# First attention of a four-layer chain: two heads share 128 rows, batches see only their own keys, query norms turned one tile later

## What is computed

```python
q = (hidden @ q_proj_w.T)   # 32 heads of 128
k = (ctx @ k_proj_w.T)      # 8 key/value heads of 128
v = (ctx @ v_proj_w.T)
q = rmsnorm(q, q_norm_w); k = rmsnorm(k, k_norm_w)       # per head
scores = einsum('bhqd,bhkd->bhqk', q, repeat(k, 4)) * scale + attention_mask
attn = softmax(scores)
out = einsum('bhqk,bhkd->bhqd', attn, repeat(v, 4))
return out @ o_proj_w.T
```

## Time and profile before

| | us |
|---|---|
| median of 3 runs | 2617.65 (2617.49 to 2620.02) |
| span of the profiled execution | 2617.0 |
| first attention in it, first projection matmul to last x update | 79.6 to 737.8 |
| TensorE busy, share of the span | 88% |
| VectorE, ScalarE, GpSimd busy | 52%, 45%, 20% |
| granted TensorE clock, mean of the span | 0.954 |

### The profile page before, as it was taken

One profiled execution on the slowest core, in us unless ns is written; L12 is line 12 of the kernel. 1 busy time (PEld: TensorE's weight loads), 2 busy tenths in 40 slices (PEclk: granted clock), 3 DMA queues, 4 the chain that ended last, 5 costly groups with the idle time before them and its releaser, 6 DMA issues.

```text
span 2617.0 us, 40130 instructions
## 1 busy us (share of the span) xinstructions
PE 2310.4 (88%) x14092; PEld 1295.4 (49%) x14108; DVE 1352.7 (52%) x2614; ACT 1167.1 (45%) x2986; POOL 530.5 (20%) x875
## 2 busy tenths in 40 slices
PE   0789989899977777999999999999769899999979
PEld 0455555555543333455555555555534455555545
DVE  2466666666652024465555565555342455555551
ACT  2455556565511112554554554543122555555530
POOL 1233332332220001122222222211200111221120
PEclk9999999999978888999999999999879999999988
DMA  3111011010000111111111111100210010000000
GB/s 126 35 41 42 22 42 37 26 41 17 1 21 14 83 71 50 59 59 43 61 60 43 61 60 43 61 11 11 77 64 1 33 49 33 32 32 32 1 29 33
DMA packets 27172, 108.74 MB, mean 42 GB/s; under 512 B 4305, under 2 KB 12881, under 8 KB 16866
## 3 DMA queue, kind: packets, MB, share of 16 engines
q1 hardware_dynamic: 26978, 106.24, 11.5%
HBM read 104.13 MB, written 2.10 MB: 41 GB/s over the span
## 4 chain that ended last, share of the span: by engine, by line
PE 58%; ACT 15%; DVE 14%; issue 10%; POOL 1%; DMA 1%; ACTq 0%; DVEq 0%; POOLq 0%; SPq 0%
PE bank L84 14%; PE bank L85 14%; PE bank L86 14%; DVE m_Sm L785 2%; ACT m_E L409 2%; PE bank L1222 2%; DVE m_x L831 2%; PE bank L1551 2%; ACT m_E L405 2%; PE bank L579 2%; ACT m_arena L387 2%; DVE m_nmax L801 1%; ACT m_arena L297 1%; PE bank L1131 1%; PE bank L1336 1%
## 5 line engine op out<-in xcount | busy, mean ns | idle before, releaser
L725 DVE TENSOR_TENSOR m_arena<-bank,m_arena 128x512 f16<-128x512 f32 x336 | 232.1, 691 | 541.6 <-ACT m_arena L387 541.2
L84 PE MATMUL bank<-m_input_parts,m_arena 128*128 128x512 f16 x1088 | 416.8, 383 | 9.5 <-DVE m_input_parts L694 2.8
L85 PE MATMUL bank<-m_input_parts,m_arena 128*128 128x512 f16 x1088 | 416.4, 383 | 0.4 <-issue 0.4
L86 PE MATMUL bank<-m_input_parts,m_arena 128*128 128x512 f16 x1088 | 416.4, 383 | 0.0
L409 ACT ACTIVATE m_E<-m_Sm,m_nmax 128x128 f32<-128x128 f32 x512 | 199.1, 390 | 427.4 <-DVE m_nmax L801 251.6
L843 POOL TENSOR_TENSOR m_E<-m_E,m_rinv 128x512 f32<-128x512 f32 x192 | 199.9, 1041 | 917.6 <-DVE m_rinv L816 917.6
L84 PE MATMUL bank<-m_wo_t,m_A 128*128 128x512 f16 x768 | 295.0, 384 | 34.5 <-DVE m_x L831 34.5
L387 ACT ACTIVATE m_arena<-bank 128x512 f16<-128x512 f32 x336 | 198.9, 592 | 243.7 <-PE bank L86 243.3
L85 PE MATMUL bank<-m_wo_t,m_A 128*128 128x512 f16 x768 | 294.3, 383 | 0.0
L86 PE MATMUL bank<-m_wo_t,m_A 128*128 128x512 f16 x768 | 293.6, 382 | 0.0
L405 ACT ACTIVATE m_E<-bank,m_nmax,m_qk 128x128 f32<-128x128 f32 x256 | 113.8, 454 | 195.1 <-DVE m_nmax L774 195.1
(11 more groups left out here) (258 smaller groups left out, 4454.5 us busy)
## 6 DMA issues: line engine op xcount, KB each, us to landing
m_raw<-a_q SPq DMA_DIRECT2D x24, 1024.0 KB, 4.8
m_raw<-a_o SPq DMA_DIRECT2D x24, 1024.0 KB, 4.9
m_raw<-a_k SPq DMA_DIRECT2D x9, 1024.0 KB, 4.9
m_raw<-a_v SPq DMA_DIRECT2D x9, 1024.0 KB, 5.4
m_bias_in<-bias SPq DMA_DIRECT2D x64, 128.0 KB, 2.0
m_arena<-ctx_t SPq DMA_DIRECT2D x3, 2048.0 KB, 7.8
m_arena<-f_w SPq DMA_DIRECT2D x4, 1024.0 KB, 5.1
m_arena<-ctx SPq DMA_DIRECT2D x1, 2048.0 KB, 8.1
```

The lines of the kernel that those rows point to most:

```text
L84: pe.matmul(out, lhs[0], rhs[0], start=first, stop=False)
L85: pe.matmul(out, lhs[0], rhs[1], start=False, stop=False)
L86: return pe.matmul(out, lhs[1], rhs[0], start=False, stop=last)
L725: ins = dve.tensor_tensor(self.dest(name, part, 1), self.shaped(bank[m % 2][:, :]), self.dest(name, part, 0), ALU.subtract)
```

## The change

In the first attention two heads of one batch share the 128 rows of a score block, and each block has only the 64 keys of its own batch. A unit then has four blocks of 128 by 64 (two batches by two pairs of heads) in place of four of 128 by 128. Queries, their squares and the mixed output are laid out by batch and pair of heads, as the last attention already does it (`self.packed`). The mask is 128 by 64. Two transposes are made in place of four. The values lie in two copies, each with zeros in the rows of the other batch, and the mix is two products of 256 columns. The value tile is split by two operations of 64 rows on ScalarE and on VectorE. GpSimd clears the values once in the setup; the mask's two loads no longer wait. And in the list of events `q_turn` moves behind the slot's `tile`.

```diff
@@ events
             if normed == 3:
-                out.append(("q_turn", misc, slot // 4))
-                misc += 1
                 out.append(("k_scale", slot // 4))
             if todo:
                 out.append(("tile", todo.pop(0), slot // 4))
+            if normed == 3:
+                out.append(("q_turn", misc, slot // 4))
+                misc += 1
@@ ScalarE, tile
+                    if self.layer == 0 and name[0] == "V":
+                        for q in range(2):
+                            own = slice(q * S, (q + 1) * S)
+                            ins = act.activation(k.V[own, 0, part, q, :], src[own, :], ACT.Copy)
+                        ins.then_inc(s["proj_hi"].sem, 1)
+                        continue
@@ ScalarE, scores and turn
-                        cols = slice(h * P, (h + 1) * P)
+                        cols = slice(h * self.keys, (h + 1) * self.keys)
-                    act.activation(k.PT[:, b % 2, 0, :], bank[4][:, :], ACT.Copy).then_inc(s["turned_hi"].sem, 1)
+                    act.activation(self.pt_dst(b, 0), bank[4][:, 0:self.keys * HG], ACT.Copy).then_inc(s["turned_hi"].sem, 1)
@@ TensorE, scores
+                        if self.packed:
+                            b2, hp = (j // 2, j % 2) if self.layer == 3 else (j % 2, j // 2)
                             lhs = [k.q3[:, i, hf, hp, pt * 2 + b2].rearrange("p h n -> p (h n)") for i in range(2)]
+                                rhs = [k.K[:, i, hf, 0, (pt * 2 + b2) * S:(pt * 2 + b2 + 1) * S] for i in range(2)]
-                        ins = mm3(pe, out[:, j * P:(j + 1) * P], lhs, rhs)
+                        ins = mm3(pe, out[:, j * self.keys:(j + 1) * self.keys], lhs, rhs)
@@ TensorE, turn and mix
-                    for j in range(4):
+                    for j in range(self.keys * HG // P):
                         ins = pe.transpose(bank[4][:, j * P:(j + 1) * P], k.E[:, b % 2, j * P:(j + 1) * P], k.ident[:, :])
-                        lhs = [k.V[:, i, hf, 0, pt * P:(pt + 1) * P] for i in range(2)]
-                        ins = mm3(pe, out[:, :], lhs, [pt_[:, i, :] for i in range(2)])
+                        for b2 in range(2):
+                            lhs = [k.V[:, i, hf, b2, pt * P:(pt + 1) * P] for i in range(2)]
+                            ins = mm3(pe, out[:, b2 * HG * S:(b2 + 1) * HG * S], lhs, [pt_[:, i, 0:HG * S] for i in range(2)])
@@ VectorE, tile
+                    elif self.layer == 0 and name[0] == "V":
+                        for q in range(2):
+                            own = slice(q * S, (q + 1) * S)
+                            ins = dve.tensor_tensor(k.V[own, 1, part, q, :], bank[m % 2][own, :], k.V[own, 0, part, q, :],
+                                                    ALU.subtract)
+                        ins.then_inc(s["proj_lo"].sem, 1)
@@ VectorE, scores
-                        for h in range(HG):
-                            cols = slice(h * P, (h + 1) * P)
-                            i = (b % 4) * HG + h
+                        for j in range(HG):
+                            cols = slice(j * S, (j + 1) * S)
+                            own = (b % 4) * 2 + j % 2
+                            i = (own % 4) * HG + (j // 2) * 2 + own // 4
@@ Setup
-        sp.wait_ge(*s["fill"].by(3))
+            sp.dma_start(k.mask0[q * S:(q + 1) * S, :], d["mask"]).then_inc(s["mask"].sem, 16)
+        pool.memset(k.V[:, :, :, 0:2, :].bitcast(FP32), 0.0).then_inc(s["fill"].sem, 1)
```

More of the change, by code:

```diff
@@ L131, in __init__ @@
         self.ahead = layer != 0
+        self.packed = layer != 2
+        self.keys = S if layer == 0 else P
     def events(self, t):
@@ L426, in dest @@
     def dest(self, name, part, i):
-        if self.layer == 3:
+        if self.packed and name[0] == "Q":
             h = int(name[1])
@@ L431, in dest, with shaped, squared, score_bank @@
         return self.k.dest(name, part, i)
-    def shaped(self, src):
-        return src.rearrange("p (b n) -> p b n", b=8) if self.layer == 3 else src
+    def shaped(self, name, src):
+        return src.rearrange("p (b n) -> p b n", b=8) if self.packed and name[0] == "Q" else src
+    def squared(self, h):
+        return self.k.qsq[:, h // 2, :, h % 2, :], self.k.q_parts[:, 0, h // 2, :, h % 2, :], self.k.q_parts[:, 1, h // 2, :, h % 2, :]
+    def score_bank(self, b):
+        return self.k.bank[2 + b % 2][:, 0:HG * self.keys]
+    def pt_dst(self, b, part):
+        return self.k.PT[:, b % 2, part, 0:self.keys * HG]
     def mix_src(self):
-        if self.layer == 3:
+        if self.packed:
             return self.k.bank[5][:, :].rearrange("p (b h n) -> p b h n", b=2, h=HG)
@@ L539, in emit @@
                     pe.wait_ge(*s["proj_lo"].by(at(t, 2 * self.NT, self.NT * part + HG)))
-                    for h in range(HG):
+                    for row in range(HG):
                         for i in range(2):
-                            ins = pe.matmul(bank[7][:, :], k.select[:, h, :], k.q_parts[:, i, h, :],
-                                            start=h + i == 0, stop=h + i == HG)
+                            moving = k.q_parts[:, i, row // 2, (row % 2) * 4:(row % 2) * 4 + 4, :, :]
+                            ins = pe.matmul(bank[7][:, :], k.select[:, row, :], moving.rearrange("p b h n -> p (b h n)"),
+                                            start=row + i == 0, stop=row + i == HG)
                     ins.then_inc(s["misc"].sem, 1)
@@ L556, in emit @@
                     pe.wait_ge(*(s["exped"] if self.layer == 3 else s["biased"]).by(at(t, 8, b - 1)))
-                    out = bank[2 + b % 2]
+                    out = self.score_bank(b)
                     if b % 4 == 0:
@@ L723, in emit @@
                         dve.tensor_copy(k.kraw[:, :], bank[m % 2][:, :]).then_inc(s["proj_lo"].sem, 1)
+                    elif self.layer == 0 and name[0] == "V":
[4 more added lines that the diff above has]
+                        ins.then_inc(s["proj_lo"].sem, 1)
                     else:
-                        ins = dve.tensor_tensor(self.dest(name, part, 1), self.shaped(bank[m % 2][:, :]),
+                        ins = dve.tensor_tensor(self.dest(name, part, 1), self.shaped(name, bank[m % 2][:, :]),
                                                 self.dest(name, part, 0), ALU.subtract)
                         if self.layer == 0 and name[0] == "Q":
-                            h = int(name[1])
-                            ins = dve.tensor_tensor(k.q_parts[:, 1, h, :], k.qsq[:, h, :], k.q_parts[:, 0, h, :],
-                                                    ALU.subtract)
+                            full, high, low = self.squared(int(name[1]))
+                            ins = dve.tensor_tensor(low, full, high, ALU.subtract)
                         ins.then_inc(s["proj_lo"].sem, 1)
@@ L767, in emit @@
                     dve.wait_ge(*s["scores"].by(at(t, 8, b + 1)))
-                    src = bank[2 + i2]
+                    src = self.score_bank(b)
                     if self.layer == 3:
@@ L800, in emit @@
                     dve.wait_ge(*s["biased"].by(at(t, 8, b + 1)))
[L801 to L802 removed]
+                    Sm = k.Sm[:, i2, 0:HG * self.keys].rearrange("p (h n) -> p h n", h=HG)
+                    ins = dve.tensor_reduce(k.nmax[:, i2, :], Sm, AX.X, ALU.max, negate=True)
                     if self.layer == 2:
@@ L819, in emit @@
                     dve.wait_ge(*s["turned_hi"].by(at(t, 8, b + 1)))
-                    dve.tensor_tensor(k.PT[:, b % 2, 1, :], bank[4][:, :], k.PT[:, b % 2, 0, :],
+                    dve.tensor_tensor(self.pt_dst(b, 1), bank[4][:, 0:self.keys * HG], self.pt_dst(b, 0),
                                       ALU.subtract).then_inc(s["turned_lo"].sem, 1)
@@ L1575, in sp @@
         sp.dma_start(k.small[:, 9:10], d["kn"]).then_inc(s["norms"].sem, 16)
-        sp.wait_ge(*s["fill"].by(3))
         for q in range(2):
-            rows = slice(q * S, (q + 1) * S)
-            sp.dma_start(k.mask0[rows, rows], d["mask"]).then_inc(s["mask"].sem, 16)
+            sp.dma_start(k.mask0[q * S:(q + 1) * S, :], d["mask"]).then_inc(s["mask"].sem, 16)
     def act(self, act):
```

34 lines of the change are left out of this document (17 added, 17 removed).

## The result

The changed kernel takes 2639.68 us (median of 4 runs, 2637.51 to 2642.28), the kernel before 2618.25 beside it. The ratio is 1.0077, 95% interval 1.0065 to 1.0090: slower by 0.8%. The forecast was 2631 us and slower, its range 2603 to 2645. The profiled execution has a span of 2635.7 us against 2617.0.

What follows compares the result with a forecast made beforehand. ScalarE and VectorE working in turn were taken to set the pace, with TensorE beside them. 2617.0 - 7.6 (chain) + 21 (clock) = 2630.4, plus 0.65 for the runs' median: 2631 us, range 2603 to 2645.

Steps and rivals of the forecast that it cites:

- The moved step: Slot 3: query-norm copies queue behind the value tile's low half, delaying the key transposes; slot 3 2.61 us longer.
- rival 1: Key transposes in slot 3: TensorE's new idle stretches don't lower the clock; 2610 us, faster; chance 0.18.
- Narrower operations: Score, maxima, exponential and PT operations on fewer columns: 0.98 us saved in slots 0 and 1, 1.03 in 2, 0.54 in 3.
- Rival 4: Narrow operations: fixed cost carries them, 64 columns last as long as 128; 29 us taken back, 2660 us; chance 0.08.
- Slot 3: Last slot of a half, with key transposes, mix and output: from 7.45 to 10.06 us, before any clock loss.
- R: End of the maxima in slot 3; key transposes were to start at R + 4.15 instead of R + 1.0.
- The clock: Behind TensorE's 3.4 to 3.8 us idle stretch in slot 3: fall to half speed costs 1.4 us, fifteen times, +21 us.
- The halves' sum: Fifteen halves of the first attention: -0.26 us each on the chain, -3.9 together, plus 21 us for the clock.
- The first half before any scores: Start of the first attention: longer wait but nothing narrower, between 0 and 2.6 us, taken as 1.3.
- Drain: Last four units, without projections: narrower scores, maxima, exponentials and PT save 1.25 us a unit, -5.0 us.
- Rival 2: TensorE's idle stretches in slot 3: half of them lower the clock; 2621 us; chance 0.14.
- rival 3: Slot 3: VectorE reaches the query-norm copies no later than before; 36.0 us a half, 2560 us; chance 0.07.

Runs made afterwards that it cites:

- e8: The changed kernel with the value tile evicted behind slot 3's mix on ScalarE and VectorE, TensorE's order untouched: 2571.56 us, ratio 0.9821 to the kernel before.
- e3: The changed kernel with 18 extra 512-column matmuls, result unused, on TensorE ahead of the key transposes: 2616.65 us, ratio 0.9990 to the kernel before.
- e2: The kernel before with only the query norms' turn moved behind the value tile: 2685.61 us, ratio 1.0246 to the kernel before.
- e4: The changed kernel with the value tile evicted by one operation instead of two on ScalarE and VectorE, batches mixed, for timing only: 2608.36 us, ratio 0.9952.
- e7: The changed kernel with query norms turned ahead of the value tile, and that tile evicted behind the mix on ScalarE and VectorE: 2576.02 us, ratio 0.9841.
- e5: The changed kernel with 8 extra 512-column matmuls, output unused, on TensorE ahead of the key transposes: 2639.12 us, ratio 1.0075 to the kernel before.

## Why the prediction was right, and where it was off

*The side and the mechanism.* The chain named in "The moved step" (exponentials, value tile high, value tile low, query-norm read, key transposes) is the one in the timeline of slot 3, and e8 shows it by taking one link out. That the clock falls behind it was the forecast over rival 1; e3 shows its price. Two readings of the rows behind this were incomplete. In the stretch of the earlier trace rows ScalarE waits for TensorE twice and not once, for 0.2 us and once for 2.4 (its copy of the query norms, L396), which changes nothing. And a second idle stretch beside the 2.68 us one kept the clock, 2.59 us at 495.28, so rival 1 had two rows for it.

*Narrower operations.* Predicted -0.98, -0.98 and -1.03 us in slots 0 to 2, with +0.12 for the layout over the half; measured -0.97, -0.96 and -1.01, which leaves 0.05 for the layout. Per operation: scores 275 ns (343 in the earlier trace rows; 68 less, where the slope said 67), maxima 420, an exponential 336. Rival 4, that fixed cost carries them, is out.

```profile
L817 DVE SCALAR_TENSOR_TENSOR m_Sm<-bank,m_rq,m_mask 128x64 f32<-128x64 f32 x212 | 45.1, 275 | 5.3 <-issue 5.3
L834 DVE TENSOR_REDUCE m_nmax<-m_Sm 128x4 f32<-128x256 f32 x53 | 22.3, 420 | 1.8
L753 DVE TENSOR_TENSOR m_arena<-bank,m_arena 64x512 f16<-64x512 f32 x26 | 17.9, 689 | 26.0 <-ACT m_arena L395 25.9
```

(Groups by line over 150 to 700 us: count, busy us, mean ns, idle time before.)

*Slot 3.* Predicted 10.06 us without the clock; e3, the same chain at full clock, has 10.49. The missing 0.43 us are in three places of the working, each read from the timeline of slot 3 with R at 392.04. ScalarE's second high half starts 0.59 after the first, not 0.48, so VectorE begins at R + 2.58 instead of R + 2.45. The two low halves take 1.42, not 1.22: 0.61 for each was a distance between starts, but here the second starts 0.70 after the first and the read of bank 7 0.73 after that, each only when the one before has ended. And the two reads with the hand-over take 0.57, not 0.49. (The recorded terms of that last step don't give its R + 4.15: 343.69 to 344.03 and 0.06 are 0.40 us and lead to R + 4.06. The 0.49 is right if the second copy is taken to its end at 344.12.) 15 x 0.43 is 6.5 us. On both engines the duration, 0.58 and 0.69, would have been nearer than the distance between starts.

*The clock.* Predicted 1.4 us a half, 21 in all; measured 1.53 a half (e3 against the changed kernel), 23. As a bound, 1.67 us (3.3 us at half speed) was too low: the changed kernel's halves lose 1.4 to 1.7 us against e3's 4.60, but the first, with 6.8 us at the low clock, loses 2.5, and e2's behind 4.22 us of idle time lose 2.3 to 2.9. The idle stretch was given as 3.4 to 3.8 us, and is 4.43. The 3.8 assumed short score matmuls, and short they are; to it come the 0.43 us above, and 0.2 us more that were not followed up. The 64-column score matmuls start every 29 ns instead of every 56:

```profile
388.32 0.19 PE L84 MATMUL bank<-m_arena 128*128 128x64 f16 x1
388.35 0.19 PE L85 MATMUL bank<-m_arena 128*128 128x64 f16 x1
388.38 0.19 PE L86 MATMUL bank<-m_arena 128*128 128x64 f16 x1
```

A unit's twelve take 0.35 us, each matmul with its own weight load; that is the most that the prediction allowed them to save. Of the two rules that the Trainium skill gives in "TensorE: Matmul & The Clock Gate" (section on the back-to-back issue gap), this is columns over 2.4 GHz plus 2.5 ns. Its other figure, about 81 ns for 128 columns in a stream of loads and matmuls, isn't seen here, where the value tile's matmuls of 128 columns start every 56 ns.

*The halves' sum.* Predicted +17.1 us for 15 halves, measured +27.5. The 10.4 us between them are slot 3, +6.5; the clock, +1.4 (22.4 us between the slots 3 of the two profiled executions, this kernel's and e3's); and slot 0 of the first half, which ran partly at the low clock and took 11.16 us instead of 9.56, where a saving was predicted, +2.5. *The first half before any scores* was put at +1.3; the first score step came 0.7 us earlier instead (111.52 against 112.24). In the profiled executions of all the kernels here it comes anywhere from 109.0 to 113.5, so neither this delay nor the clearing of V can be read from it. GpSimd's power for the query norms (the third line of the waits) starts with the key transposes and is done 3 us before the next scores, covered as the prediction said, with the slower clock's help. *Drain:* predicted -5.0, measured -3.25 in three slots (4.82 instead of 5.90 each) and -1.1 from the last scores on. *The rest of the kernel,* which the change doesn't touch, took 1875.5 us instead of 1879.2 in the profiled execution. In sum 27.5 - 0.7 - 4.4 - 3.7 = 18.7 us, where the prediction had 13.4. The median of the runs went up by 21.4. So the mechanism was right and the halves' sum too small by 10.4 us, and it is partly luck that the profiled total is off by only half of that: the start (+1.3 forecast, -0.7 measured) and the untouched rest (-3.7) gave 5.7 us back.

*The range and the rivals.* Rival 2 (some falls) is what e4 did, and rival 3 (the read of bank 7 not late, 36.0 us a half, 2560) is what e7 and e8 were built to be; they reach 36.7 and 36.8. Rival 3's sum had no term for the split value tile, which every variant pays; in the changed kernel its second operations cost 1.43 us a half (e4). That they are also what e7 and e8 lack to 36.0 is likely from e7's timeline, but no run has their order with an unsplit tile.

## What to carry over

When a step is moved past another in a list that all engines share, look up for each engine what its own operation of that step now stands behind, and whether that one waits for a third engine. It can be enough to move the event on one or two engines: here eviction order alone was worth 68 us, with TensorE's order unchanged. And a wait of TensorE that comes right ahead of the only stretch in which it is the bound has to be priced twice, once as a wait and once at the lower clock.

## What the runs showed of the hardware

The length of an idle stretch of TensorE did not settle whether the clock falls. Counted over the halves of one execution each: 4.43 us, always (the changed kernel, with 5.01 in its first half and 3.70 and 2.58 in its last two, which fell too); 4.22, always (e2); 2.71, always, and 1.97 once of once, while 0.86 kept it (e5); 3.01, three times in twelve (e4), where 3.58 fell and 2.27 and 1.16 kept it; 0.94, never (e8). In the kernel before, 2.68 and 2.59 us in this attention kept it, and five of six stretches of 2.2 to 2.3 us in the last attention lost it. In e4 the fall came 1 us after the work had begun, in the changed kernel within 0.5 us of its first instruction on either side, and in e2 1.3 us ahead of it in the half shown. So where the stretch lies in time seems to count as well as its length; this was not tried by itself and stays open. That 2.68 us kept the clock was no ground for any threshold.

How long the low clock lasts isn't fixed by the stretch either: 3.4 us at 4.43 us of idle time, 6.8 us at 4.22 (e2).

An operation on 64 of the 128 partitions costs what one on all of them does: 689 ns on VectorE and 583 ns on ScalarE for 512 columns, as the full ones in the earlier trace rows (0.69 us and 582 ns). Splitting an eviction by rows doubles it.
